# A conv-attention-experts kernel: four edits to its prologue, and matmuls without a reader on TensorE between the first products

## The reference

```python
x = x + conv(groupnorm(x))          # a DCT-weighted sum per channel, two small gates, a scale per channel
t = tokens(x)                       # 1024 tokens of 128 channels per image
t = t + attention(layernorm(t))     # 8 heads of 16; a second branch with a fixed exponential kernel over positions
t = t + experts(layernorm(t))       # top 2 of 8 experts per token, hidden size 256
```

## Time and profile before

| | us |
|---|---|
| median of 3 runs | 2345.14 |
| lowest, highest | 2336.59, 2345.91 |
| profiled execution | 2341.54 |
| its span in the trace | 2339.6 |
| busy: PE, DVE, ACT, POOL | 2030.3, 1838.9, 1471.9, 1021.9 |

### The profile page before, as it was taken

How to read it: one execution, slowest core, us unless ns; L and a number is a source line. 1 busy time by engine, 2 the same in 40 slices (tenths; PEclk the granted TensorE clock), 3 DMA queues, 4 the chain that set the end, 5 groups by cost and what they waited for, 6 DMA issues and landing times.

```text
span 2339.6 us, 34275 instructions
## 1 busy us (share of the span) xinstructions
PE 2030.3 (87%) x11456; PEld 895.6 (38%) x11456; DVE 1838.9 (79%) x2613; ACT 1471.9 (63%) x2913; POOL 1021.9 (44%) x1479
## 2 busy tenths in 40 slices
PE   2688999999999999999999999999999367887844
PEld 1233333333333333333333333333333156666633
DVE  5768798998989899898989899898971356766632
ACT  1137787878777787877778787777775134444420
POOL 2101234434343443534344353433324546777764
PEclk9999999999999999999999999999996579999975
DMA  5320322323142222314122231412012178667659
GB/s 173 58 49 1 55 47 47 91 39 78 24 84 40 53 53 41 72 25 88 35 58 52 42 69 27 90 28 57 16 51 92 64 231 291 218 203 214 205 171 341
DMA packets 100982, 215.00 MB, mean 92 GB/s; under 512 B 30224, under 2 KB 50392, under 8 KB 100376
## 3 DMA queue, kind: packets, MB, share of 16 engines
q1 hardware_dynamic: 78000, 166.96, 29.2%
q0 software_dynamic: 17280, 35.95, 4.4%
q10 hardware_dynamic: 5528, 9.91, 1.3%
HBM read 104.30 MB, written 61.23 MB: 71 GB/s over the span
## 4 chain that ended last, share of the span: by engine, by line
PE 58%; DVE 16%; POOL 9%; DMA 6%; issue 5%; ACT 4%; ACTq 1%; SPq 1%; POOLq 0%; DVEq 0%
PE ps L905 25%; PE ps L917 18%; DVE row_max L1460 10%; POOL y_dram L783 7%; ACT region L1208 2%; DMA region<-y_dram 2%; PE ps L881 2%; DMA y_dram<-region 2%; DMA big<-w_dram 2%; DVE region L1506 2%; PE ps L867 2%; PE ps L936 2%; PE ps L871 2%; PE ps L859 1%; PE ps L925 1%
## 5 line engine op out<-in xcount | busy, mean ns | idle before, releaser
L1460 DVE TENSOR_REDUCE row_max<-ps 128x1 f32<-128x1024 f32 x1024 | 1236.9, 1217 | 169.6 <-PE ps L881 150.5
L1208 ACT ACTIVATE region<-ps 128x512 f32<-128x512 f32 x2048 | 1101.0, 600 | 348.5 <-PE ps L905 338.0
L905 PE MATMUL ps<-big 50*128 50x512 f32 x2048 | 830.9, 471 | 40.8 <-ACT region L1208 22.7
L881 PE MATMUL ps<-big 48*128 48x512 f32 x2048 | 832.3, 473 | 37.2 <-DVE row_max L1460 22.2
L905 PEld LDWEIGHTS ps<-big 50*128 50x128 f32 x2048 | 337.8, 189 | 744.6 <-ACT region L1208 345.9
L917 PE MATMUL ps<-region 128*32 128x512 f32 x4096 | 564.7, 625 | 0.0
L881 PEld LDWEIGHTS ps<-big 48*128 48x128 f32 x2048 | 339.5, 192 | 76.3 <-DVE row_max L1460 57.2
L783 POOL DMA_INDIRECT y_dram<-region x284 | 272.8, 960 | 117.3 <-issue 82.9
L729 POOL DMA_INDIRECT xs_dram<-region,slot x256 | 250.0, 977 | 81.1 <-issue 71.8
L665 POOL TENSOR_TENSOR norm_v<-norm 128x8 f32<-128x8 f32 x32 | 6.7, 211 | 613.5 <-DVE norm L1450 613.5
L1053 PE MATMUL ps<-big 128*128 128x512 f32 x284 | 125.9, 443 | 69.7 <-DMA big<-w_dram 69.0
(11 more groups left out here) (185 smaller groups left out, 1945.6 us busy)
## 6 DMA issues: line engine op xcount, KB each, us to landing
big<-w_dram SPq DMA_DIRECT2D x71, 514.0 KB, 4.7
big<-q_parts SPq DMA_DIRECT2D x384, 64.0 KB, 2.4
big<-k_parts SPq DMA_DIRECT2D x372, 64.0 KB, 2.4
region<-xs_dram SPq DMA_DIRECT2D x71, 264.0 KB, 2.9
region<-y_dram SPq DMA_DIRECT2D x16, 1024.0 KB, 10.0
region<-in_x SPq DMA_DIRECT2D x28, 512.0 KB, 5.2
t_dram<-region SPq DMA_DIRECT2D x16, 512.0 KB, 3.4
out<-region ACTq DMA_DIRECT2D x16, 512.0 KB, 6.2
```

What stands on the lines that cost most here:

```text
L881: mm = pe.matmul(ps[:, M_BANK + 2 * (n % 2) + c, :], lane_rows(q_stack[k % 2], h, SHIFT_ROW)[:, t * P:(t + 1) * P], lane_rows(k_stack[k % ...
L905: pe.matmul(ps[:, bank, :], lane_rows(k_stack[k % 2], h, STACK)[:, t * P:(t + 1) * P], lane_rows(q_stack[k % 2], h, STACK)[:, c * BANK:(c ...
L1208: act.activation(probs[:, u % 2, step_head(k, s, i), :], ps[:, bank, :], ACT.Exp, scale=DH ** -0.5).then_inc(exp_done, 1)
L1460: dve.tensor_reduce(row_max[:, h * TILES + t:h * TILES + t + 1], ps[:, at:at + 2, :], AX.XY, ALU.max).then_inc(max_done, 1)
```

## The change

Six things are done.

1. The four loads of ones move from ScalarE's queue to SyncE's, behind its ninth image load.
2. Image 0's normalisation moves from GpSimd to ScalarE: GpSimd computes 1/sqrt(variance) and, in two further small operations, minus the mean times it; ScalarE applies both in eight activations.
3. Image 0's four q and k projections get banks 2 to 5, one each, in place of bank 7, and wait for the eviction of their own half of the normalised tokens alone.
4. Image 0's v and z products move from steps 27 to 30 to steps 34 to 37 of the first pass, behind the turn of the maxima.
5. `keep_busy(16)`: sixteen matmuls of 128x128 by 512 columns in fp32, whose results nobody reads, go into bank 0 between the projections and the first maxima.
6. One such matmul follows each unit of the first pass in a step that has no preparation work, and two follow the last of the moved z products.

```diff
 AT_BACKWARD = (30, 32, 34, 36, 38, 40, 42, 44)
 AT_MAX0 = 57
 AT_MAX0_FIRST = 33
+BUSY_STACKS = 16
 AT_TURN_T2 = (19, 21)
 AT_LOGITS, AT_TURN_L = 23, 29
 AT_TURN_O = (31, 47, 53)
 AT_VZ = (45, 51, 59, 61)
-AT_VZ_FIRST = (27, 28, 29, 30)
+AT_VZ_FIRST = (34, 35, 36, 37)
 AT_DISPATCH = 49
 
 AT_COPY_O = (17, 33, 49)
...
         bn1_done = sem("bn1_done")
         bn2_done = sem("bn2_done")
         n1_done = sem("n1_done")
+        rows0_done = sem("rows0_done")
         n2_done = sem("n2_done")
         qk_split = sem("qk_split")
         q_high = sem("q_high")
...
                 return LANE_HEADS * i + s % 2
             return LANE_HEADS * (s % 2) + i
 
+        def projection_bank(kind, k, c):
+            return side(kind, k, c) if k else ps[:, M_BANK + HALVES * ("q", "k").index(kind) + c, :]
+
         block = ctx.enter_context(nc.Block())
 
         @block.sync
...
             for tile, name in consts[:FROM_SP]:
                 sp.dma_start(tile, a[name]).then_inc(const_in, 16)
             for n, k in enumerate(X_LATER):
+                if n == STREAM:
+                    sp.wait_ge(ones_done, 1)
+                    for rows in ones_rows:
+                        sp.dma_start(rows.rearrange("p h (n c) -> p (h n) c", c=P).bitcast(F32),
+                                     ones_r[:, :].bitcast(F32).unsqueeze(1).broadcast_to([PARTS, HEADS // LANES * TILES, P])
+                                     ).then_inc(late_in, 16)
                 if n >= STREAM:
                     sp.wait_ge(stats_done, FIRST + n - STREAM + 1)
                 sp.dma_start(stream_buf[n % STREAM], a["x"][k]).then_inc(stream_in[n % STREAM], 16)
...
             link(pool.memset(n2_row[:, :, P:ROW], 0.0))
             inverse_root(0)
 
-            def normalise(tok, n):
+            def moments(n, shift=False):
                 v = norm_v[:, n]
                 even, odd, s_even, s_odd = (norm6[:, n, :, c] for c in (1, 4, 2, 5))
                 pool.tensor_tensor(v[:, 0, :], even, odd, ALU.add)
...
                 link(pool.tensor_tensor(v[:, 5, :], v[:, 5, :], v[:, 2, :], ALU.add))
                 link(pool.tensor_scalar(v[:, 6, :], v[:, 5, :], 1.0 / P, 1e-5, ALU.mult, ALU.add))
                 link(pool.tensor_tensor(v[:, 7, :], v[:, 6, :], minus_half[:, 0:TILES], ALU.pow))
+                if shift:
+                    link(pool.tensor_scalar(v[:, 1, :], v[:, 0, :], -0.5, None, ALU.mult))
+                    pool.tensor_tensor(v[:, 1, :], v[:, 1, :], v[:, 7, :], ALU.mult).then_inc(rows0_done, 1)
+
+            def normalise(tok, n):
+                v = norm_v[:, n]
+                moments(n)
                 if n:
                     pool.sem_inc(rs2_done, 1)
                 for row, op in ((3, ALU.subtract), (7, ALU.mult)):
...
                 tag(k, 1)
                 send(1)
 
-            norm1(0)
+            pool.wait_ge(bn1_done, 1)
+            moments(0, shift=True)
             pool.wait_ge(late_in, LATE_INC)
             for it in range(-1, IMAGES + 1):
                 if 0 <= it < IMAGES:
...
                 mm.then_inc(side_ready, 1)
 
             def project(kind, k, c, w):
-                take_side(kind, k, c)
-                pe.matmul(side(kind, k, c), w[:, :], norm_ch[k % 2][:, c * BANK:(c + 1) * BANK], start=True,
+                if k:
+                    take_side(kind, k, c)
+                else:
+                    pe.wait_ge(side_free, side_at["back_n", 0, c] + 1)
+                pe.matmul(projection_bank(kind, k, c), w[:, :], norm_ch[k % 2][:, c * BANK:(c + 1) * BANK], start=True,
                           stop=True).then_inc(side_ready, 1)
 
             def values_and_z(k, b):
...
                                lane_rows(k_stack[k % 2], h, SHIFT_ROW)[:, c * BANK:(c + 1) * BANK], start=True, stop=True)
                 if c == HALVES - 1:
                     mm.then_inc(full_ready, 1)
+
+            def keep_busy(products):
+                for _ in range(products):
+                    pe.matmul(ps[:, RING[0], :], wq[:, :], norm_ch[0][:, 0:BANK], start=True, stop=True)
 
             def turn_maxima(k, g):
                 pe.wait_ge(max_done, k * STEPS + (g + 1) * GROUP_ROWS)
...
             for c in range(HALVES):
                 project("k", 0, c, wk)
             pe.wait_ge(setup_done, 2)
+            keep_busy(BUSY_STACKS)
             for it in range(-1, IMAGES + 1):
                 here, nxt, prep, post = 0 <= it < IMAGES, it + 1 < IMAGES, it + 2 < IMAGES, it >= 1
                 at_turn, at_back, at_q, at_k = (AT_PREP_FIRST, AT_PREP_LATE, AT_PREP)[min(it + 1, 2)]
...
                     for c in range(HALVES):
                         if post and s == AT_OUT[c]:
                             project_out(it - 1, c)
+                    if it < 0 and units and not any(s in at for at in (at_turn, at_back, at_q, at_k, at_vz)):
+                        keep_busy(1)
                     if nxt and s == at_max0:
                         turn_maxima(it + 1, 0)
                     if it == IMAGES - 1 and s == AT_BIAS:
...
                         turn_o(it, AT_TURN_O.index(s))
                     if nxt and s in at_vz:
                         values_and_z(it + 1, at_vz.index(s))
+                    if it < 0 and s == at_vz[-1]:
+                        keep_busy(2)
                     if post and s == AT_DISPATCH:
                         dispatch(it - 1)
 
...
                 if name == "b_gate":
                     src = src.unsqueeze(0).broadcast_to([P, TILES, EXPERTS])
                 act.dma_start(tile, src).then_inc(late_in, 16)
-            act.wait_ge(ones_done, 1)
-            for rows in ones_rows:
-                act.dma_start(rows.rearrange("p h (n c) -> p (h n) c", c=P).bitcast(F32),
-                              ones_r[:, :].bitcast(F32).unsqueeze(1).broadcast_to([PARTS, HEADS // LANES * TILES, P])
-                              ).then_inc(late_in, 16)
 
             def excite():
                 lo, hi = ROUNDS[0]
...
                     act.wait_ge(qk_split, 2 * k)
                     for g in range(GROUPS):
                         act.wait_ge(stack_in[(k - 1) % 2][g], ((k - 1) // 2 + 1) * STACK_INC)
-                act.activation(parts[:, 0, c * BANK:(c + 1) * BANK], side(kind, k, c), ACT.Copy).then_inc(q_high, 1)
+                act.activation(parts[:, 0, c * BANK:(c + 1) * BANK], projection_bank(kind, k, c), ACT.Copy).then_inc(q_high, 1)
                 q_highs[0] += 1
                 act.wait_ge(q_high, q_highs[0])
-                act.activation(dst[:, c * BANK:(c + 1) * BANK], side(kind, k, c), ACT.Copy).then_inc(side_free, 1)
+                act.activation(dst[:, c * BANK:(c + 1) * BANK], projection_bank(kind, k, c), ACT.Copy).then_inc(side_free, 1)
 
             def vz_out(k, b):
                 act.wait_ge(side_ready, side_at["vz", k, b] + 1)
...
             for c in range(HALVES):
                 x_out(0, c)
             affine(1)
+            act.wait_ge(rows0_done, 1)
+            for t in range(TILES):
+                last = act.activation(x_tok[:, t, :], x_tok[:, t, :], ACT.Identity, scale=norm_v[:, 0, 7, t:t + 1],
+                                      bias=norm_v[:, 0, 1, t:t + 1])
+            last.then_inc(n1_done, 1)
             for c in range(HALVES):
                 norm_out(0, c)
             for c in range(HALVES):
```

## The result

The change makes the kernel slower: median 2387.84 us (2382.86 to 2394.43, four runs) against 2343.60 (2336.59 to 2345.91, four), a ratio of 1.0169 [1.0123, 1.0214]. Forecast were 2325 and a gain. The profiled execution took 2394.43, its span is 2392.5, and its mean granted clock is 0.910 where it was 0.944.

A forecast was written before the change was run, and what follows sets the result against it. TensorE at its lower clock to 182 us, behind one chain through all engines before the first scores, was taken as the bound; -10.2 + 0 + 4.2 - 12.2 = -18.2 from 2341.5 gave 2323.3, stated as 2325, range 2312 to 2340.

The forecast's parts named there:

- Sixteen dense products: Between projections and first scores: they end at 64.9 with one slow product, so the first score starts 10.2 us earlier.
- better: Rival, chance 0.12: the clock rises among the projections and a full 14 is gained at both ends; -24, 2318 us.
- image 0's first sixteen steps: Steps behind the first scores: at the higher clock level 32.9 us against 45.1, 12.2 less (0 if the clock is lost).
- Products among the maxima: First maxima, one product in 26 of 34 steps: 56.6 us at the higher level against 56.67, nothing gained.
- hidden: Rival, chance 0.10: products overrun the stacks by five or six slow products' worth, a half-score takes 0.46; -6, 2336 us.
- the clock never rises: Rival, chance 0.14: products are pure cost; first score 4.6 late, maxima 47.8 more, wait 9.7 more; 62 slower, 2403 us.
- The wait behind the maxima: From the turn of the maxima to image 0's first score, with v and z moved there: 9.8 and a handoff, 4.2 more.
- rises and is lost again: Rival, chance 0.18: the clock drops in the v and z products or image 0's first steps; -8, plus 2, 2335 us.
- The prologue: Start to the k split: 4.0 + 4.1 + 0.7 + 4.1 = 12.9 us earlier; the first score could start at 62.2.
- First Exp: ScalarE, ones loads moved to SyncE: from 21.8 to 17.05 (4.7 us) or 18.35 (3.4), by table load order; 4.0 taken.
- The activations: Image 0's normalisation on ScalarE: eight activations take 3.0 us (2.2 to 4.8), 3.7 with the rest in place of 7.82.
- The k split: VectorE, before the stack loads: due at 48.6, with its statistics done in time.

The follow-up runs named there:

- experiment 1: The changed kernel with 22 instead of 16 dense products ahead of the stacks; 2347.16 us, 0.9955 of the kernel before.
- experiment 5: The changed kernel with its sixteen dense products held back until a later VectorE statistic, so that they end behind the stacks; 0.9964 of the kernel before.
- experiment 10: The changed kernel with 19 instead of 16 dense products ahead of the stacks; 2334.62 us, 0.9934 of the kernel before.
- experiment 6: The changed kernel with 22 products ahead of the stacks and 256 instead of 512 columns per product among the maxima; 0.9955 of the kernel before.
- experiment 7: As experiment 6, plus one half-width product in each of image 0's first twelve steps; 0.9973 of the kernel before.
- experiment 9: As experiment 6, plus one full-width product in each of image 0's first twelve steps; median 2334.74 us, 0.9930 of the kernel before.
- experiment 8: As experiment 6, plus one full-width product in each of image 0's first six steps; 0.9899 of the kernel before.
- experiment 3: The prologue's four changes alone: no unread products anywhere, v and z back at steps 27 to 30; 2335.32 us, 0.9931 of the kernel before.
- experiment 2: The changed kernel without the products among the first maxima, the other unread products kept; 2331.25 us, 0.9908 of the kernel before.

## Why the prediction was wrong, point by point

**The step that failed is "Sixteen dense products": the overlap of their end with the stacks.** It let them overrun the stacks: from 47.35, 1.04 us each and one slow, to 64.9, with the stacks at 62.2. The stacks came at 62.40. The products began at 44.47, because the clock rose among the projections already, took 0.87 each, none of them slow, and ended at 58.37, 6.5 early (2.9 from the start, 2.7 from the sixteen, 0.9 from the slow one). The "better" rival counted that early rise as a gain, and neither asked what TensorE does in the hole behind a run that ends too soon. The hole of 4.03 us cost the clock, and with it the next two terms of the sum, the maxima and the wait. A second step failed as well, image 0's first sixteen steps, below.

**Products among the maxima.** The sum for the higher level, 56.6, was right: 56.45 in experiments 1, 5 and 10, with a slot of 0.66 for a pair of scores (63.10 to 63.76 in experiment 1), not the 0.92 of the rival "hidden". At the lower level the rival "the clock never rises" had 47.8 us more and was right too: 46.5. It named the wrong cause (the clock did rise) and so added a late first score that didn't come; its 2403 is nearer to 2387.84 than the forecast.

**The wait behind the maxima.** Forecast 9.8 and a handoff; 9.52 where the clock held, 14.17 where not (v and z at 2.07 each from 167.07 on; the rival had 15.4).

**Image 0's first sixteen steps.** 12.2 us less were forecast; measured were 0.7 less in after, 3.8 in experiment 1, 0.4 in 6, and 12.4 more in 7 (57.47). What failed is the condition, a clock that holds; no run shows these steps at the higher level without added products, so the size of the term stays unmeasured. In after, 1 and 6 the steps begin at the higher level and TensorE then idles 0.92 to 0.93 us, once, for VectorE's part of the excitation chain (184.68 in after); within 1.3 us the durations are those of the lower level. Experiment 7 lost the clock beside shorter waits (0.32), and experiment 9 kept it beside one of 0.33, so the waits aren't shown to be the cause. In one execution of each, the runs show that the clock went there without added products and with half-width ones, and held where full-width ones stood (8 and 9). The cause stays open. The rival "rises and is lost again" named this place. So even where the gap is closed the products give no more than the prologue: 0.9955, 0.9964 and 0.9934 in experiments 1, 5 and 10 against 0.9931 in 3; the forecast, 2325 of 2343.60, was 0.992.

**The prologue.** Its sum, 12.9, is near the 12.7 measured, but by luck: misses cancel. First Exp: 18.66; the first small product started 1.6 us later than before in this execution, so the edit itself gave 4.7, the upper of the two values, since the table load ran at 12.14 ahead of the activation's wait. The activations: 3.19 where 3.0 was taken. The Trainium skill (ScalarE: Activation LUTs, section "What ACT_TABLE_LOAD costs") led to an estimate of 3.2, and the trace agrees with 3.19. The k split began at 46.48, 2.1 earlier than forecast. But ScalarE took 11.57 us to issue the twelve stack loads, 3.9 more than before, where up to 2 was allowed; 9.64 in experiment 3, without dense products. What lengthens it wasn't tried.

## What to carry to other kernels

Filler that is to raise a clock ahead of a wait has to last until the wait ends in every execution: too short by 4 us it cost 55 us here (1.0169 against experiment 10's 0.9934, of some 2350), because more filler, priced for the higher level, stood behind it. Filler inside a stage is bought with the clock: at the lower level the same products cost double (2.07 against 1.05) and raised nothing, so ask first what happens if the clock isn't there. And time a bundle's parts alone: the prologue's edits are worth 0.7%, and no version with filler is measurably better: the intervals of experiments 2, 8, 9 and 10 overlap with that of 3, though all five beat both kernels.

## What the runs showed of the hardware that was not expected

- A stretch can be busy for all of 103.19 us and stay at a clock of 0.50, while the same instructions, entered at 1.00, stay there for 56.45: this mix held a level and didn't raise it.
- The clock rose among four fp32 projections of 128x512 back to back: in after the two of q take 2.99 together, the two of k 1.88. In experiment 3, with the same code, they take 3.62 and 2.68, so where it rises differs between executions.
- Such a product takes 0.87 us in a dense run at the higher level, and 1.05 between 48-row scores (63.76 to 64.81 in experiment 1).
- The clock column reads 1.00 in before's maxima, 0.50 for the same durations in experiment 3: ahead of a first recorded change it isn't to be trusted.
- The same code takes different times: the stretch behind the last turn, which no experiment edits, took 587.0 to 611.2 us in the twelve profiled executions, at mean clocks of 0.82 to 0.77. Experiment 8's profile, in which v and z lost the clock that they kept in 6, 7 and 9, shows the same on a small scale. What decides either stays open.
